# Bias matmuls with 128 rows of weights in place of three, in a graph network layer

## The reference

```
h = maximum(layernorm(x), 0)                       # 6250 x 128
for t in 0..2:                                     # three edge types
    msg = relu(h[src] @ W_e[t].T + b_e[t])         # zero where edge_type != t
    parts[t] = segment_sum(msg, dst)               # 6250 x 128
agg = concat([relu(h), parts[0], parts[1], parts[2]])
updated = where(node_type == t, agg @ W_n[t].T + b_n[t])
out = x + updated + h
```

## Time and profile before

| | |
|---|---|
| median of three runs | 1382.92 us |
| lowest, highest | 1382.15, 1385.01 us |
| the profiled execution | 1379.95 us |
| its span, first to last instruction | 1378.1 us |
| TensorE matmuls busy | 1321.6 us, 96% |
| GpSimd busy | 985.2 us, 71% |
| VectorE busy | 1066.4 us, 77% |
| ScalarE busy | 521.3 us, 38% |
| mean granted TensorE clock | 0.984 |

### The profile page before, as it was taken

How to read it: one execution, slowest core, us unless ns; L and a number is a source line. 1 busy time by engine, 2 the same in 40 slices (tenths; PEclk the granted TensorE clock), 3 DMA queues, 4 the chain that set the end, 5 groups by cost and what they waited for, 6 DMA issues and landing times.

```text
span 1378.1 us, 26300 instructions
## 1 busy us (share of the span) xinstructions
PE 1321.6 (96%) x9037; PEld 1016.6 (74%) x9037; DVE 1066.4 (77%) x3638; ACT 521.3 (38%) x1027; POOL 985.2 (71%) x1042
## 2 busy tenths in 40 slices
PE   7877999999999999999999999999999999999976
PEld 2436888888788877888877877788777777777753
DVE  6789988888888778888898888787768767767621
ACT  4865443344344334433443443333233323323300
POOL 2337777777777777777777777777777777777772
PEclk9998999999999999999999999999999999999997
DMA  8563322232332263223223322622222222222221
GB/s 265 192 184 109 85 77 74 74 90 75 89 92 78 56 209 91 79 74 92 70 72 92 93 60 70 200 59 59 71 64 60 70 71 64 65 65 66 64 69 37
DMA packets 94690, 124.84 MB, mean 91 GB/s; under 512 B 20786, under 2 KB 72486, under 8 KB 94557
## 3 DMA queue, kind: packets, MB, share of 16 engines
q0 software_dynamic: 31744, 65.08, 18.1%
q1 hardware_dynamic: 61935, 57.05, 13.1%
q10 hardware_dynamic: 878, 1.02, 0.2%
HBM read 97.38 MB, written 25.68 MB: 89 GB/s over the span
## 4 chain that ended last, share of the span: by engine, by line
POOL 46%; PE 33%; issue 15%; DMA 3%; DVE 2%; ACT 1%; POOLq 0%; DVEq 0%; SPq 0%; ACTq 0%
POOL rows L556 45%; PE ps L724 13%; PE ps L708 8%; PE ps L686 5%; PE ps L743 2%; PE ps L616 2%; DMA message_table<-work 2%; DMA rows<-message_table,idx 1%; PE ps L741 1%; PE ps L614 1%; DVE arena L1116 0%; PE ps L602 0%; DVE work L1222 0%; PE ps L740 0%; DMA work<-message_table 0%
## 5 line engine op out<-in xcount | busy, mean ns | idle before, releaser
L556 POOL DMA_INDIRECT rows<-message_table,idx x992 | 960.8, 969 | 315.2 <-issue 298.7
L874 ACT CAST arena<-ps 128x490 f16<-128x490 f32 x828 | 430.5, 573 | 731.8 <-PE ps L708 731.4
L724 PE MATMUL ps<-mem,arena 128*120 128x384 bf16 x3381 | 622.8, 327 | 1.4 <-DVE mem L1227 1.4
L724 PEld LDWEIGHTS ps<-mem,arena 128*120 128x120 f16 x3381 | 435.2, 133 | 107.6 <-issue 4.5
L1116 DVE TENSOR_SCALAR arena<-iota_j,jkey 128x441 bf16<-128x441 f16 (+2 forms) x1656 | 444.5, 330 | 37.0 <-PE ps L708 34.7
L708 PE MATMUL ps<-arena,lhot 128*128 128x441 bf16 (+3 forms) x2484 | 353.6, 277 | 8.5 <-DVE lhot L1128 4.3
L686 PEld LDWEIGHTS ps<-onehot,rows 128*128 128x128 f32 x1984 | 251.2, 194 | 39.4 <-DMA rows<-message_table,idx 23.7
L1128 DVE TENSOR_TENSOR lhot<-ps,lkey 128x512 bf16<-128x512 f32 x412 | 278.4, 676 | 0.0
L1197 DVE TENSOR_TENSOR acc<-ps,acc 128x60 f32 (+1 forms) x455 | 94.0, 207 | 229.0 <-PE ps L686 187.0
L686 PE MATMUL ps<-onehot,rows 128*128 128x27 f32 x1984 | 247.4, 265 | 21.6 <-DMA rows<-message_table,idx 16.9
L708 PEld LDWEIGHTS ps<-arena,lhot 128*128 128x128 bf16 x2484 | 192.2, 99 | 78.4 <-DVE lhot L1128 5.0
(11 more groups left out here) (121 smaller groups left out, 396.8 us busy)
## 6 DMA issues: line engine op xcount, KB each, us to landing
rows<-message_table,idx POOLq DMA_INDIRECT x992
message_table<-work SPq DMA_DIRECT2D x49, 192.0 KB, 1.9
work<-message_table SPq DMA_DIRECT2D x21, 448.0 KB, 4.5
kept_planes<-work SPq DMA_DIRECT2D x14, 672.0 KB
mem<-kept_planes SPq DMA_DIRECT2D x14, 672.0 KB, 5.6
own_hT<-work SPq DMA_DIRECT2D x49, 64.0 KB, 1.7
work<-own_hT SPq DMA_DIRECT2D x49, 64.0 KB
xr<-in_x_dram SPq DMA_DIRECT2D x48, 64.0 KB
```

The lines of the kernel that those rows point to most:

```text
L556: pool.indirect_dma_start(out=rows[:, g % SLOTS, u, :], out_offset=None, in_=table_rows, in_offset=bass.IndirectOffsetOnAxis(ap=idx[:, g, ...
L724: m = pe.matmul(psQ[q % 2][0:BW * SL, 0:3 * D], counts[q % 2][:, c * MC + e, :], planes[:, c * MC + e, :, :].rearrange("p v d -> p (v d)") ...
L874: act.copy(counts[q % 2][:, :, a:a + PC], psB[m % 3][:, 0:HB * PC].rearrange("p (w h) -> p h w", w=PC)).then_inc(d_count, 1)
```

## The change

The three tiles get 128 partitions. `ones` is 128x128 and all ones; `be_all` and `bn_all` are 128x384, set to zero by two new memsets at the start of VectorE's program; `three_rows` writes the parts of the bias to their first three rows. The 125 other rows add ones times zero. The matmuls at L612, L614, L740 and the one in the fallback at L784 (which this input does not enter) take the whole tiles. No instruction is moved, and nothing else is added or taken away; 98 matmuls and 98 weight loads that run have 128 rows where they had three.

```diff
-        be_3 = sb("be_3", [3, TD], BF16)
-        bn_3 = sb("bn_3", [3, TD], BF16)
-        ones = sb("ones", [3, P], BF16)
+        be_all = sb("be_all", [P, TD], BF16)
+        bn_all = sb("bn_all", [P, TD], BF16)
+        ones = sb("ones", [P, P], BF16)
...
-                    pe.matmul(psH[s][:, 0:TD], ones[:, :], be_3[:, :], start=False, stop=True).then_inc(tab_mm, 1)
+                    pe.matmul(psH[s][:, 0:TD], ones[:, :], be_all[:, :], start=False, stop=True).then_inc(tab_mm, 1)
                     return
-                pe.matmul(psH[s][:, 0:TD], ones[:, :], be_3[:, :], start=True, stop=False)
+                pe.matmul(psH[s][:, 0:TD], ones[:, :], be_all[:, :], start=True, stop=False)
...
-                pe.matmul(psF[:, 0:TD], ones[:, :], bn_3[:, :], start=True, stop=False)
+                pe.matmul(psF[:, 0:TD], ones[:, :], bn_all[:, :], start=True, stop=False)
...
             dve.memset(ones[:, :], 1.0)
+            dve.memset(be_all[:, :], 0.0)
+            dve.memset(bn_all[:, :], 0.0)
...
-            three_rows(0, be_3[:, :]).then_inc(bias_ok, 1)
+            three_rows(0, be_all[0:3, :]).then_inc(bias_ok, 1)
...
-            three_rows(1, bn_3[:, :])
+            three_rows(1, bn_all[0:3, :])
```

## The result

| | before | changed |
|---|---|---|
| median, five runs each | 1384.55 us | 1376.28 us |
| ratio, 95% interval | | 0.9935 (0.9907 to 0.9962) |
| the profiled execution, its span | 1378.1 us | 1371.1 us |
| the changed kernel measured again, twelve runs | 1382.21 us | 1377.29 us |
| ratio, 95% interval | | 0.9966 (0.9952 to 0.998) |

The account below looks back on a forecast made before the run. GpSimd's 992 gathers set the pace from 91.41 us, so TensorE's speed matters only in the table and tail. Gains of 2.9 and 0.6 us sum to 3.5, from 1382.92 to 1379.4 us, range 1375.8 to 1384.2.

Parts of the forecast that it names:

- What one bias matmul costs: Table and finishing blocks on TensorE: exposed weight loads around the 3-row matmul cost 0.30 us a block, three times 0.10.
- The first rival: The row count does nothing; data type switch or semaphore makes the gaps around the bias matmul; 1382.9 us, chance 0.12.
- Table before 42 us, 0, and the memsets: Early table blocks wait for stores, new memsets are covered: 0, bounds 1.2 us won and 0.8 us lost.
- Table, 42 to 70 us, 0: 18 table blocks: TensorE's lead only becomes a stall ahead of block 39, since VectorE works without a break; 0 won.
- a lead of 5.4 us: TensorE up to 18 x 0.30 us ahead by table block 35, turning into a stall ahead of block 39.
- Table, 70 to 88 us, 2.9: ReLUs of table blocks 35 to 47: VectorE's waits for TensorE vanish and VectorE becomes the bound; 2.9 us won.
- the second rival: Half the gain comes back at the VectorE stretch, through late transposes or low clock after the stall; 1381 us, chance 0.10.
- The 0.3 us for transposes: Taken off the 70 to 88 us gain: block 44's transposes start only when VectorE has emptied their PSUM tile.
- Gathers, 0: All 992 gathers shift with the table's gain; finishing steps beside them are hidden, so nothing on top.
- Tail, 0.6: Behind the last gather: about 0.3 us from a half-clock finishing step and 3 x 0.10 from three more; 0.6 us won.
- the sum: Table 2.9 plus tail 0.6 us: 3.5 us won, profiled execution from 1379.95 to 1376.4, forecast 1379.4 us against 1382.92.

Follow-up runs that it names:

- the memsets alone: Changed kernel with its 128-row tiles and memsets, but three rows used in all bias matmuls; ratio 1.0003 (0.9983 to 1.0023) to the kernel before.
- The finishing matmuls alone: Changed kernel with three rows again in the table, so 128 rows stand in finishing only; ratio 0.9996 (0.998 to 1.0012) to the kernel before.
- changed again: The changed kernel run once more, unaltered, for a second trace and set of times; ratio 0.9966 to the kernel before.
- table alone: Changed kernel with three rows again in finishing, so 128 rows stand in the table only; ratio 0.9967, median 1378.71 us against 1382.21 before.
- both fillings: Changed kernel plus extra matmuls in TensorE's stall behind table block 41 and ahead of the tail's last groups and steps; ratio 0.9927, median 1372.9 us against 1382.19 before.
- the tail's alone: Changed kernel plus 12 extra matmuls ahead of the last gathered groups but one, 6 ahead of last finishing steps; ratio 0.9954 to the kernel before.

## Why the prediction was wrong, point by point

*What one bias matmul costs*: right. 0.30 us a block, all three gaps of 0.10 closed, and the Trainium skill's column rule for loads ("TensorE: Matmul & The Clock Gate", "LDWEIGHTS (loading the stationary operand)") did not decide: the loads themselves take 0.09 us for 3 rows and 0.10 for 128, as that rule has it, but the cost lay in when a load may start. L616's first pass went from 590 to 486 ns. The first rival falls: with 96 rows, still bf16 between fp32, the loads are hidden.

*Table before 42 us, 0, and the memsets*: right. The landing varies from 39.1 to 42.4 us, 40.8 in the mean of either kind of kernel, and the memsets alone measured 1.0003.

*Table, 42 to 70 us, 0*: **this step failed.** I read from one execution that VectorE's first ReLU waited only 0.22 us, and took it for the rule. In three of six executions with exposed loads TensorE was 2.7 to 8.2 us late there, after 14 to 24 us at half clock, in two 0.2 us late, and in one it was 0.6 us ahead. With hidden loads it was late in none of seven, and 0.7 to 3.4 us ahead. A table that comes 0.22 us late has no reserve; that the change gives it one is shown by these thirteen traces. That the reserve is worth 2.5 us in the mean rests on three long executions, and a split of three in six against none in seven would come by luck once in fourteen times. I had computed a lead of 5.4 us, and counted it only as a stall.

*Table, 70 to 88 us, 2.9*: **this step failed too**, and it was the main term. 14.3 us were forecast from ReLU 35 to ReLU 47 (14.0 of VectorE and 0.3 of waiting). It was 16.5 to 17.8 with hidden loads against 16.7 to 17.1 with exposed ones, no gain in the mean, and 15.65 in the one trace at full clock whose fillings fit the stall. Three terms were mis-sized. The clock (the second rival, which I had given 0.10) took 1.3 us in the changed kernel's own trace: 17.77 against 16.46 where only one low stretch fell there. The 0.3 us for transposes that can't start in time was 1.17. TensorE can't run ahead of VectorE, since the transposes of keys behind block 41 wait for VectorE to empty a tile, and the blocks 42 to 44 with their transposes come after it. The wait at the low bits is 1.18 us before, 1.13 after and 1.17 with the clock full. And VectorE's own share is 14.3 to 14.5 us, not 14.0: of the 0.68 us that the ReLU of block 39 waited before, 0.32 stay in every kernel with hidden loads, for VectorE's own reduction (L1159), which was no wait for TensorE.

*Gathers, 0*: right in the mean. The finishing matmuls alone measured 0.9996; the 3.1 us of the first pair of traces are within the spread of 1258.8 to 1266.4.

*Tail, 0.6*: too small for the pair of traces, and not contradicted by the medians. One part can be read off: a step at full clock was 4.43 us and is 4.23, since L741's two passes take 0.65 us of the chain where they took 0.84, so that 0.20 us is won a step where 0.10 was forecast. The rest of its length goes roughly with the clock that was granted behind 1325 us: 20.3 us with 11.4 us at half clock (changed again), 24.1 with 23.9 (table alone), 24.8 with 20.5 (before). The kernel with both fillings has 20.2, the one with the tail's alone 21.2 with 3.4 us low, so that the clock isn't all of it.

*The two traces as a pair*: I set the sum against one profiled execution 3 us below the median of its kernel, and the size of a gain of some us can't be read from one pair when single executions differ by more. The two terms that failed have opposite signs: some 2.5 us won where I had 0, none where I had 2.9. That 4.7 us in twelve runs isn't far from 3.5 is luck.

What stays open: why the clock was low so much longer between 20 and 70 in some executions with exposed loads, where 2.2 of the 4.7 us come from, and what changes between 64 and 69 rows so that a load may start early.

## What to carry to other kernels

A matmul with few rows of weights between full ones can cost two weight loads that would otherwise be hidden; padding it with zeros to 96 or 128 rows left the matmul itself at 0.33 us and gave 0.30 us each here. Whether that shortens the kernel depends on who is ahead: look for the stretch in which the engine has no reserve, in more than one execution, not only for its idle time in one. Where the faster engine then stalls, ask what clock it comes back with; filling the stall and the tail with matmuls nobody needs brought perhaps another 0.4% here, in six runs, and only where the filling ended with the stall.

## What the runs showed of the hardware

- Bias matmuls of 3, 32 and 64 rows of bf16 weights between 128-row ones: 0.26 us to the next matmul and 590 ns for it. 96 and 128 rows: 0.16 us and 486 ns. The bias matmul itself takes 0.33 us in all.
- Matmuls of 69 rows (fp32, 69 columns) between 128-row ones: at full clock the load on either side starts 1 to 5 ns after the start of the matmul ahead (66 to 80 ns behind the last such set in the kernels with hidden loads).
- The Trainium skill, "TensorE: Matmul & The Clock Gate", section "The mechanism", lets a load overlap running matmuls only where their row groups differ. The rows differ from this sentence: loads of 128 rows were hidden under matmuls of 69, 96, 120 and 128 rows, and exposed between 128 rows and 64 or fewer. The same section of the Trainium skill also lets a load to the background weight buffer go ahead; that fits the hidden ones, and says nothing of 64 rows.
- TensorE, 2.09 us busy of 4.00 from 70 to 74, had the clock fall to 0.50 at 75.2 and came back at that; with the stall filled by 20 matmuls of 384 columns the clock stayed at 1.00 from 72 to 88, in two traces.
- The identity on VectorE at the start hid two memsets of 128x384 (0.22 us each): what follows it starts at 5.92 us before and after, as the earlier trace rows had suggested.
